# AdaLN feed-forward, two layers, one core: where the small head is issued, and which engine scales, adds and masks

## What is computed

```
layer 0:
  y[b,e]  = mean of x[b,e,t] over t < length[b]          # masked mean
  gate    = sigmoid(conv5(y) over e)                     # x gated by rows
  h       = silu(q(x*gate) @ ternary(w_gate).T) * (q(x*gate) @ ternary(w_up).T)      # 512 -> 1376
  x1      = x + q(h) @ ternary(w_down).T                 # q: 127-level rounding by the row's max
layer 1:
  delta   = 0.5 * lora_B @ lora_A
  v       = (weight + delta) / exp(scale_log)            # scale per row and block of 128
  w_eff   = codebook[searchsorted(thresholds, v)] * exp(scale_log) + delta           # 512 x 512
  out     = x1 + (x1 @ w_eff.T) @ W_base.T + b + softmax-weighted adapters of the chosen 4 of 16 experts
```

## Time and profile before

| | |
|---|---|
| median of 3 runs | 153.93 us (153.88 to 154.12) |
| the profiled execution's own time | 153.92 us |
| its span in the trace | 152.10 us |
| TensorE matmul | 138.4 us busy, 91% |
| TensorE weight load | 84.7 us, 56% |
| VectorE | 114.1 us, 75% |
| ScalarE | 96.1 us, 63% |
| GpSimd | 11.0 us, 7% |
| mean granted TensorE clock | 0.989 of full |

### The profile page before, as it was taken

One profiled execution on the slowest core, in us unless ns is written; L12 is line 12 of the kernel. 1 busy time (PEld: TensorE's weight loads), 2 busy tenths in 40 slices (PEclk: granted clock), 3 DMA queues, 4 the chain that ended last, 5 costly groups with the idle time before them and its releaser, 6 DMA issues.

```text
span 152.1 us, 2134 instructions
## 1 busy us (share of the span) xinstructions
PE 138.4 (91%) x661; PEld 84.7 (56%) x661; DVE 114.1 (75%) x302; ACT 96.1 (63%) x156; POOL 11.0 (7%) x31
## 2 busy tenths in 40 slices
PE   6779999998799967898579999999999999999993
PEld 2256665753356544446234545454576766797792
DVE  2799999989999999999978856998996031035561
ACT  3799998996997975965365659797663403400200
POOL 7000000000000033200004200000000000000000
PEclk9999999999999999999968999999999999999999
DMA  5999999849600430603100905150400000000193
GB/s 172 336 402 421 419 414 404 323 130 396 225 0 0 86 45 5 129 0 69 26 0 0 166 2 107 22 97 2 95 0 4 0 0 0 4 0 0 63 377 112
DMA packets 19486, 19.22 MB, mean 126 GB/s; under 512 B 13474, under 2 KB 13858, under 8 KB 19476
## 3 DMA queue, kind: packets, MB, share of 16 engines
q1 hardware_dynamic: 19476, 19.10, 39.8%
HBM read 13.82 MB, written 2.10 MB: 105 GB/s over the span
## 4 chain that ended last, share of the span: by engine, by line
PE 50%; DVE 27%; ACT 10%; issue 8%; DMA 2%; SPq 0%; ACTq 0%; DVEq 0%
PE bank L971 15%; PE bank L918 12%; ACT tern_d L526 6%; PE bank L881 6%; PE bank L887 6%; DVE hmax L1322 5%; DVE raw_gate L1319 4%; PE bank L929 3%; DVE junk L1158 2%; DMA cond<-in_cond_w 2%; DVE rmax L1208 2%; ACT cond L492 2%; PE bank L978 1%; DVE tern_i L1203 1%; PE bank L863 1%
## 5 line engine op out<-in xcount | busy, mean ns | idle before, releaser
L881 PE MATMUL bank<-tern_g,head_sb 128*128 128x464 bf16 (+1 forms) x96 | 22.6, 357 | 1.0 <-DVE tern_u L1204 0.8
L887 PE MATMUL bank<-tern_u,head_sb 128*128 128x464 bf16 (+1 forms) x96 | 22.5, 357 | 0.6 <-DVE raw_gate L1319 0.6
L918 PE MATMUL bank<-tern_d,delta 128*128 128x512 bf16 (+1 forms) x88 | 22.0, 399 | 0.5 <-DVE tern_d L1204 0.5
L971 PE MATMUL bank<-m_h,fr 128*128 128x512 f32 (+1 forms) x72 | 22.3, 378 | 0.0
L1319 DVE TENSOR_TENSOR raw_gate<-bank,wbt 128x464 f32<-128x464 f32 (+1 forms) x24 | 15.1, 631 | 4.2 <-ACT wbt L624 3.7
L624 ACT ACTIVATE wbt<-bank,s_g 128x464 f32<-128x464 f32 (+1 forms) x24 | 14.9, 633 | 3.4 <-PE bank L881 3.3
L1322 DVE TENSOR_REDUCE hmax<-raw_gate 128x1 f32<-128x464 f32 (+1 forms) x24 | 15.1, 631 | 0.8
L631 ACT ACTIVATE raw_gate<-raw_gate,hq 128x1376 int16<-128x1376 f32 x8 | 11.5, 1438 | 6.5 <-DVE hq L1329 6.5
L918 PEld LDWEIGHTS bank<-tern_d,delta 128*128 128x128 bf16 (+1 forms) x88 | 9.0, 103 | 11.5 <-issue 1.9
L887 PEld LDWEIGHTS bank<-tern_u,head_sb 128*128 128x128 bf16 x96 | 9.3, 98 | 10.0 <-DVE raw_gate L1319 1.2
L796 PE MATMUL bank<-wbt,cond 128*128 128x512 f32 x32 | 14.8, 599 | 0.0
(11 more groups left out here) (177 smaller groups left out, 226.8 us busy)
## 6 DMA issues: line engine op xcount, KB each, us to landing
raw_gate<-in_w_gate_t SPq DMA_DIRECT2D x4, 688.0 KB, 7.4
raw_up<-in_w_up_t SPq DMA_DIRECT2D x4, 688.0 KB, 12.3
xs<-in_x SPq DMA_DIRECT2D x8, 256.0 KB, 13.2
out_x<-xs SPq DMA_DIRECT2D x7, 256.0 KB, 2.2
raw_down<-in_w_down_t SPq DMA_DIRECT2D x2, 768.0 KB, 5.4
cond<-in_cond_w SPq DMA_DIRECT2D x4, 256.0 KB, 4.6
wbt<-in_w_base_t SPq DMA_DIRECT2D x4, 256.0 KB, 9.2
raw_down<-in_w_down_t SPq DMA_DIRECT2D x2, 512.0 KB, 7.6
```

The costliest lines, as they stand in the source:

```text
L881: mm = pe.matmul(bank_g[n % 2][:, 0:w], xq_t[:, b % 2, k, :], tern_g[:, k, f0:f0 + w], start=(k == 0), stop=(k == KH - 1))
L887: mm = pe.matmul(bank_u[n % 2][:, 0:w], xq_t[:, b % 2, k, :], tern_u[:, k, f0:f0 + w], start=(k == 0), stop=(k == KH - 1))
L918: mm = pe.matmul(bank_down[:], h_t[0:rows, b % 2, j, :], tern_d[0:rows, j, :], start=(j == 0), stop=(j == KF - 1))
L971: pe.matmul(bank_y[n_res][:, h0:h1], a[:, b, k, :], m[:, k, h0:h1], start=(n == 0), stop=False)
```

## The change

- The 36 small columns of the head become a transfer of their own, issued by ScalarE first of all; SP's first transfer holds only the lora matrices, and TensorE waits for that one.
- VectorE puts the thresholds in order, converts lengths and adapter numbers at the head, before `normalise(0)`. `normalise(0)` waits for ScalarE group by group.
- GpSimd scales blocks 1 to 3 of `cond_w` (one two-input instruction with the scale broadcast, in place of four of ScalarE), and adds delta in all four blocks (`w_eff`).
- GpSimd masks x of sequences 5 to 7 (an is_lt, then a product, each 128x512) after the fourth codebook; ScalarE sums the rows (`masked_sum`), in place of VectorE's `x_sum`.
- The three columns of `hmax` go: the maxima of the first two chunks are written right behind the hidden row, and the third reduction reads them with its chunk.
- `x_max(5, NB)` becomes three calls at other places, and m_s moves from behind chunk 1 of sequence 3 to before it.

```diff
+            act.dma_start(head_sb[:, 2 * H:HEAD], head).then_inc(ld_head, 16)
-            sp.dma_start(head_sb[:], head).then_inc(ld_head, 16)
+            sp.dma_start(head_sb[:, 0:2 * H], lora0).then_inc(ld_lora, 16)
...
+            def scaled_weight(k):
+                pool.wait_ge(inv_done, 1)
+                pool.wait_ge(ld_cond[k], 16)
+                v = cond[:, k, :].rearrange("p (g i) -> p g i", g=KH)
+                pool.tensor_tensor(v, v, scl_inv[:, k, :].unsqueeze(2).broadcast_to([P, KH, GROUP]),
+                                   ALU.mult).then_inc(condn_done, 1)
+
+            def w_eff(k):
+                pool.wait_ge(delta_done, min(k + 2, KH))
+                pool.wait_ge(value_done, k + 1)
+                pool.tensor_tensor(cond[:, k, :], cond[:, k, :], delta[:, k, :], ALU.add).then_inc(weff_done, 1)
+
+            def masked_x(b):
+                m = masked[:, b - GROUPS[2][0], :]
+                pool.wait_ge(ld_x[b], 16)
+                pool.wait_ge(len_done, 1)
+                pool.tensor_scalar(m, t_iota[:], len_f[:, b:b + 1], None, ALU.is_lt).then_inc(below_done, 1)
+                pool.wait_ge(below_done, b - GROUPS[2][0] + 1)
+                pool.tensor_tensor(m, m, xs[:, b, :], ALU.mult).then_inc(masked_done, 1)
+
+            for k in range(1, KH):
+                scaled_weight(k)
+            w_eff(0)
+            w_eff(1)
...
+            w_eff(2)
+            w_eff(3)
+            pool.wait_ge(cb_ps, KH)
+            for b in range(GROUPS[2][0], NB):
+                masked_x(b)
...
+            def masked_sum(b):
+                i = b - GROUPS[2][0]
+                act.wait_ge(masked_done, i + 1)
+                act.activation(masked[:, i, :], masked[:, i, :], ACT.Copy,
+                               accum_out=ysum[:, b:b + 1]).then_inc(xsum_done, 1)
...
                 if b == 2:
                     rounded_down(3)
+                    for i in range(GROUPS[2][0], NB):
+                        masked_sum(i)
...
+            inner_thresholds()
+            lengths()
+            outer_thresholds()
+            adapter_numbers()
             normalise(0)
-            masks(0, 0, 1)
-            ordered_thresholds()
-            masks(0, 1)
+            dve.wait_ge(th_done, 2)
+            masks(0)
...
-                link(dve.tensor_reduce(hmax[:, b % 2, c:c + 1], hs, AX.X, ALU.max, apply_absolute_value=True))
+                if c < NC - 1:
+                    row_max, src = hrow[b % 2][:, F + c:F + c + 1], hs
+                else:
+                    row_max, src = hred[:, b:b + 1], hrow[b % 2][:, f0:F + NC - 1]
+                link(dve.tensor_reduce(row_max, src, AX.X, ALU.max, apply_absolute_value=True))
...
-                link(dve.tensor_reduce(hred[:, o], hmax[:, b % 2, :], AX.X, ALU.max))
...
                 if b == 3:
-                    x_max(5, NB)
                     residual(0)
+                    dve.wait_ge(msh_done, 1)
+                    dve.tensor_tensor(ms_l, bank_ms.rearrange("p (k c) -> p k c", k=KH),
+                                      ms_h.bitcast(F32), ALU.subtract).then_inc(msl_done, 1)
                 if b < NB:
                     hidden_chunk(b, 1)
...
                     y_safe(2)
+                    x_max(7, NB)
...
                     ternary_down(4)
-                    x_sum(5)
-                    x_sum(6)
-                    x_sum(7)
+                    dve.wait_ge(xsum_done, NB - GROUPS[2][0])
                     y_mean(2)
+                    x_max(5, 6)
+                    x_max(6, 7)
```

More of the change, by code:

```diff
@@ L77, with build @@
 SUMMED_BY_ACT = 3
-def build(nc, x, head, w_gate_t, w_up_t, w_down_t, cond_w, w_base_t, b_base,
+def build(nc, x, head, lora0, w_gate_t, w_up_t, w_down_t, cond_w, w_base_t, b_base,
           lora1, router, conv_band, out):
@@ L169, in build @@
             pass
-        with nc.sbuf_tensor("raw_down", [P, KF, H], F32) as raw_down:
+        with nc.sbuf_tensor("raw_down", [P, SLOTS, H], F32) as raw_down:
             pass
@@ L173, in build @@
         mask = [mask_sb[:, i, :] for i in range(SLOTS)]
+        masked = raw_down[:, KF + 1:KF + 1 + NB - GROUPS[2][0], :]
         x1t_h = fr[:, 0:2, :].rearrange("p a (b k e) -> p (a b) k e", b=4, k=KH)
@@ L224, in build @@
         silu = wbt_flat[:, 0:2 * CHUNKS[0][1]].rearrange("p (i f) -> p i f", i=2)
-        hbuf = [raw[0][:, i * F:(i + 1) * F] for i in range(2)]
-        patterns = raw[0][:, 2 * F:4 * F].bitcast(I16)
+        hrow = [raw[0][:, i * (F + NC - 1):(i + 1) * (F + NC - 1)] for i in range(2)]
+        hbuf = [row[:, 0:F] for row in hrow]
+        patterns = raw[0][:, 2 * F + 8:4 * F].bitcast(I16)
         h_i = patterns[:, 0:2 * KF * P].rearrange("p (i f) -> p i f", i=2)
-        h_bits = raw[0][:, 2 * F:4 * F].bitcast(BF16)[:, 0:2 * KF * P].rearrange("p (i f) -> p i f", i=2)
+        h_bits = raw[0][:, 2 * F + 8:4 * F].bitcast(BF16)[:, 0:2 * KF * P].rearrange("p (i f) -> p i f", i=2)
         ht_i = patterns[:, 2 * KF * P:3 * KF * P].rearrange("p (j e) -> p j e", j=KF)
         xt_i = patterns[:, 3 * KF * P:3 * KF * P + 2 * H].rearrange("p (i k e) -> p i k e", i=2, k=KH)
-        hmax = sb("hmax", [P, 2, NC])
         hred = sb("hred", [P, NB])
@@ L297, in build @@
         qx_done = sem("qx_done")
+        len_done = sem("len_done")
+        below_done = sem("below_done")
+        masked_done = sem("masked_done")
+        xsum_done = sem("xsum_done")
         ymean_done = sem("ymean_done")
@@ L485, in _ @@
             act.activation(scl[:], slog, ACT.Exp).then_inc(scl_done, 1)
[L487 to L495, removed]
+            act.wait_ge(inv_done, 1)
+            act.wait_ge(ld_cond[0], 16)
+            for g in range(KH):
+                c = slice(g * GROUP, (g + 1) * GROUP)
+                act.activation(cond[:, 0, c], cond[:, 0, c], ACT.Copy,
+                               scale=scl_inv[:, 0, g:g + 1]).then_inc(condn0_done, 1)
             def diagonals(i):
@@ L509, in _ @@
             act.wait_ge(step_done, 1)
-            for n, i in enumerate(T_ORDER):
+            for i in T_ORDER:
                 diagonals(i)
-                if n == 3:
-                    scaled_weight(1)
             act.wait_ge(scl_done, 1)
@@ L1130, in value @@
                                          ALU.add, ALU.mult).then_inc(value_done, 1)
-            def w_eff(k):
-                dve.wait_ge(delta_done, min(k + 2, KH))
-                dve.wait_ge(value_done, k + 1)
-                dve.tensor_tensor(cond[:, k, :], cond[:, k, :], delta[:, k, :], ALU.add).then_inc(weff_done, 1)
             def lengths():
@@ L1240, in _ @@
             masks(1, 3)
-            w_eff(0)
             normalise(2)
             value(1)
-            w_eff(1)
             masks(2)
-            lengths()
             normalise(3)
@@ L1251, in _ @@
             masks(3, 4)
-            w_eff(2)
             x_sum(0)
@@ L1259, in _ @@
             y_safe(0)
-            w_eff(3)
             ternary_chunk(0, 1, rounded_by_act=2)
@@ L1452 @@
         "x": n(x),
+        "lora0": np.tile(np.concatenate([n(L1_cond_lora_A), n(L1_cond_lora_B).T], axis=1), (P // RANK0, 1)),
         "head": np.concatenate([
[L1454 removed]
             np.tile(np.concatenate([n(condB_codebook),
```

30 lines of the change are left out of this document (17 added, 13 removed).

## The result

The changed kernel takes **161.85 us** (161.46 to 162.48) beside 153.91 (153.83 to 154.12) for the kernel before on the same chip: 1.0518 times as long, 95% interval 1.0481 to 1.0554. The forecast was 150.0. The profiled execution took 162.48 us, with a span of 160.7.

What follows compares the result with a forecast made beforehand. All three big engines nearly full to 38 us, VectorE the bound to 77, TensorE after, and TensorE's matmuls also a bound in the head; 0 + 3.5 - 1.0 + 1.4 = 3.9 off 153.9 gives 150.0 us, range 147.6 to 153.3.

Steps and rivals of the forecast that it cites:

- (a): Head, up to the lora products: earlier masks' gain of 0.8 us eaten by meetings with GpSimd, taken as 0.
- Rival 4: Shared way to SBUF becomes the bound, small VectorE steps waiting too: slower, 155.2 us; chance 0.1.
- rival 3: Clock falls all the same, TensorE perhaps pausing 1.6 us near 62 us before down(0): 151.9 us; chance 0.12.
- (b): Lora products to x transposes: waits of TensorE go, a gain of 0.8 us carried into sequence 0.
- -1.0 for the meetings: Term within (c): VectorE's meetings with GpSimd's queued work, mainly 31 to 40 us, cost 1.0 us (bounds 0 and 2.5).
- (c): To the x1 transposes, VectorE-bound: they start 3.5 us earlier, 0.8 of it (b)'s, less 1.0 for meetings with GpSimd.
- (d): X1 transposes to the end: clock stays up (1.87 us), about 0.5 given back, gain 1.4 (bounds 0 and 1.9).

Runs made afterwards that it cites:

- run 9: Changed kernel with masked sums back on VectorE, GpSimd still making its three comparisons and three products into an unread tile: 161.94 us.
- Run 1: Changed kernel with blocks 1 to 3 of cond_w scaled by ScalarE again at their old places: 159.04 us.
- run 14: Kernel before with the chained maxima, m_s ahead of chunk 1 of sequence 3 and x_max(5, NB) as three calls: 152.11 us, 0.9898.
- run 13: Changed kernel with ScalarE scaling the blocks, plus three one-input GpSimd products of 128x512 into an unread tile: 157.94 us.
- run 7: Changed kernel with ScalarE scaling the blocks, plus three two-input GpSimd products of the same shape into an unread tile: 162.17 us.
- run 3: Changed kernel with delta added by VectorE again (w_eff at its old places): 161.07 us.

## Why the prediction was wrong

**The bound** was read rightly in the main: what is put on VectorE before 77 us counts. Not all that is taken off it does: run 9 puts the three sums back on VectorE at no cost that can be measured. The holds that the changed kernel's rows show come to about 9 us (2.3 in the head, 2.5 by the adds, 4.2 by the masked work), and 7.35 of GpSimd's cost reached the time, fallen clocks included.

**(a) The head, taken at 0, came out at -6.0.** Three steps failed.
- *The landing.* It was taken at 2.85 with bounds of 1.7 us after issue and 4.1; it was 4.78, outside them. The upper bound was wrong in kind: it took the small transfer to be no later than the large one that it had been a part of. By the runs, 3.9 to 4.9 beside the large loads in a second queue, 2.4 first in the same queue. That is 1.9 us of the 4.05 by which normalise(0) missed the forecast 6.6. The text also says that with the transfer at 4.1 nothing of the gain of 0.8 is left. By its own terms it is worse: 4.1+1.72+0.88+1.14 = 7.84 for normalise(0), and 12.7 for the lora products, a loss of 0.4; at 4.78 it is 1.1.
- *The meeting.* The text let one GpSimd op meet masks(0) ("only the op under way when masks(0) comes"). But its three products ran from 6.05 to 9.10 beside the small steps that the change itself had put there. They were held 2.3 us. Masks(0), at 11.81, met nobody. GpSimd's 1.15 per product was a fair size (1.02); the step that failed is who is met. Rival 4 named the small steps, at a chance of 0.1. "Each waiting for the other's instruction" was already the reading of the earlier trace rows, and nothing in it exempts a small step that waits: it should have been taken at its word.
- *The clock.* The pause before codebook(0), 1.27 us in the kernel before, became 5.87, and the fall behind it cost another 2.4. The sum had no term for a fall of the clock in the head; rival 3 had one near 62 us alone.

Run 1 parts the 6.0: without the three products, but with the late landing (4.89), codebook(0) starts at 10.27, takes 4.8 us at a fallen clock instead of 3.4, and the lora products come at 15.06. So 2.8 of the 6.0 are there without GpSimd, and the three products, with the deeper fall of the clock that they bring, add 3.2.

**(b) A gain of 0.8 from there to the x transposes came out at -0.9.** The adds hold VectorE for 2.5 us here, and s_g and the step behind it wait for the masked work. Here "-1.0 for the meetings" of the middle stretch is the mis-sized term: the six masked instructions alone cost 4.1 (run 9), outside its bound of 2.5. The comparison was taken at 0.77, the one-input row, and took 1.75 to 2.04, with VectorE's clamps beside it; the product was taken at 1.15 and took 1.27 to 1.51.

**(c) The end of the stretch was right, and its start wasn't.** ScalarE's three sums came as read: 0.61 and 0.19 each, 1.84 from the first to the silu (2.1 forecast), and VectorE waited 0.83 for it (1.1 forecast).

```profile
75.03 0.61 ACT L604 ACTIVATE raw_down<-raw_down 128x512 f32<-128x512 f32 x1
...
76.87 0.61 ACT L661 ACTIVATE wbt<-bank,s_g 128x448 f32<-128x448 f32 x1
77.39 0.67 ACT L749 ACTIVATE b_full<-bank,two_row 96x512 f32<-96x512 f32 x1
```

From the end of w_down's last clamp to the x1 transposes it is 5.2 us (80.21 to 85.42), where the text has 5.4, and the kernel before 8.0. But up to that clamp the stretch took 35.9 us (44.28 to 80.21) instead of 31.6 (37.43 to 69.02): the held clamps, waits of 1.29 and 2.24 instead of one of 0.81, a second fall of the clock near 52 us, and the 1.49 for b_full. Of that last one rival 3 had forecast 1.6, with a fall of the clock behind it; it didn't fall. Its text has no pause between 0.81 us and 2.62; the trace before has 1.31 at 54.32, without a fall.

**(d) Taken at +1.4, it came out at -0.2.** The clock stays up from the x1 transposes on, as forecast (0.60 instead of 0.89 for the four). What the text gives back, 0.5, was too small: waits of 0.68 and 0.92 follow in the changed kernel, 1.15 and 0.58 in run 14. A stage whose next engine has little room gives a gain at its start back.

**Rival 4** was the one that came in, by its mechanism, sign and place (small steps waiting, turns in the middle stretch), but at 155.2 it was still 6.7 us short: the late landing, both falls of the clock and the long comparisons weren't in it.

The Trainium skill was weighed with the GPSIMD Engine Reference, which says who contends and not for how long. Its page SBUF — State Buffer (SBUF: two separate sides) says it: the pair of ports that VectorE and GpSimd share is locked by whoever starts first, for a whole instruction, and the other blocks fully. The rows agree (0.17 became 0.88 to 1.01, to the end of GpSimd's instruction). Its section Who interferes with whom excepts VectorE's reductions and what reads at most one SBUF input outside the two-port modes; the reciprocal and normalise, one input of which is in PSUM, weren't held in run 13. The unheld two-input step at 41.04, beside a comparison, doesn't fit it.

**Open.** GpSimd's comparison took from 1.56 us (run 7, at 43.17) to 2.46 (run 3, at 40.19), where its product by two values took 0.77. In run 7's trace VectorE's two-input step 0.07 us into a comparison took 0.63 (43.24), and one 0.75 us into another took 0.16 (40.66). Why a comparison is so long, and lets some steps through, wasn't tried. Nor was the masked work at a time when VectorE waits anyway, after 77 us.

## What to carry to other kernels

Work moved to GpSimd isn't free because GpSimd is idle: where VectorE is the bound, each GpSimd instruction can hold VectorE's next one to its own end, and a step of one column pays as much as one of 512 (reciprocals, and steps that read PSUM, weren't held here); so count the instructions and lay them beside what VectorE does at that very time. A wait of some us on TensorE in a stretch where it is close to the bound costs itself and then, at a fallen clock, the work behind it, here another 2.4 us. A small transfer in a second queue isn't early because it is small: here it was early only as the first of the one queue, and then what stood behind it was late.

## What the hardware showed that was not expected

- Beside a GpSimd product of 1.02 us a VectorE step of 128x1 took 0.88 us and one of 128x4 1.01, instead of 0.17; 13 GpSimd instructions, 18.0 us by their groups (3.1 + 5.2 + 5.7 + 4.0), cost the kernel 7.35 us, fallen clocks included.
- GpSimd's comparison with a column's value took 1.91 us on the mean for 128x512 with VectorE busy beside it, and 1.56 at the least (run 7); its product by two such values took 0.77.
- 18 KB took 4.0 us to land from a second queue and 1.7 as the first of the other, issued at the same moment (0.73 and 0.72).
- A pause of 1.31 us before the same transposes was followed by a fallen clock in one kernel (rows of 1.73 instead of 0.96) and not in another; one of 1.49 wasn't either. At what length a pause costs the clock can't be told from these rows.
